# Attention scores in two fp32r parts with two heads per pass of the array, and a new order of TensorE's work

## The reference

```python
h = _layernorm(x) * (1 + ca) + sa
qkv = einsum('bsd,ed->bse', h, w_qkv) + b_qkv            # 16 heads of 16
scores = einsum('bhqd,bhkd->bhqk', q, k) / sqrt(16) + causal
attn = softmax(scores); out = einsum('bhqk,bhkd->bhqd', attn, v)
x = x + ga * (out @ w_out.T + b_out)
h = _layernorm(x) * (1 + cb) + sb
gate = h @ gate_weight.T; top1 = argmax(gate); rank = cumsum(one_hot) - one_hot   # dropped if rank >= 320
expert = gelu(dispatch @ wi) @ wo; x = x + gb * prob * expert[slot]
```

## Time and profile before

| | |
|---|---|
| median of three runs | 787.2 us (785.28 to 787.46) |
| span of the profiled execution | 782.6 us, 12208 instructions; no other time of it is given, so some 4.6 us lie around the span if it is like the median |
| first max unit, first scores unit | 41.1 us, 79.9 us |
| last max unit, last scores unit | 508.5 us, 590.9 us |
| first up matmul of the experts | 633 us |
| busy share PE, DVE, ACT, POOL | 88%, 72%, 59%, 17% |

### The profile page before, as it was taken

One profiled execution on the slowest core, in us unless ns is written; L12 is line 12 of the kernel. 1 busy time (PEld: TensorE's weight loads), 2 busy tenths in 40 slices (PEclk: granted clock), 3 DMA queues, 4 the chain that ended last, 5 costly groups with the idle time before them and its releaser, 6 DMA issues.

```text
span 782.6 us, 12208 instructions
## 1 busy us (share of the span) xinstructions
PE 689.1 (88%) x4290; PEld 367.2 (47%) x4290; DVE 561.1 (72%) x1467; ACT 459.5 (59%) x962; POOL 133.9 (17%) x194
## 2 busy tenths in 40 slices
PE   4686989999999998999999999989996279999994
PEld 3564534432323343323332323242543269999994
DVE  7754778788888787988888898960435437777762
ACT  1422445566676667766677676657783336656551
POOL 6000222220001132003310201100105300121122
PEclk9869889999999999999999999999999559999998
DMA  7436126630006033005900006000004283455200
GB/s 243 109 76 144 41 57 147 162 68 14 2 0 162 1 81 81 2 1 124 308 1 1 1 1 214 1 28 1 28 28 162 90 234 115 155 182 201 92 23 17
DMA packets 42111, 66.53 MB, mean 85 GB/s; under 512 B 3822, under 2 KB 31985, under 8 KB 41466
## 3 DMA queue, kind: packets, MB, share of 16 engines
q1 hardware_dynamic: 39746, 59.44, 27.3%
q0 software_dynamic: 2304, 6.31, 2.2%
HBM read 39.36 MB, written 26.78 MB: 85 GB/s over the span
## 4 chain that ended last, share of the span: by engine, by line
PE 74%; DVE 10%; ACT 8%; issue 4%; DMA 2%; POOL 1%; SPq 0%; DVEq 0%; POOLq 0%; ACTq 0%
PE bank L1245 17%; PE bank L1295 15%; PE bank L1325 14%; PE bank L1430 9%; PE bank L1413 8%; ACT probs L802 4%; PE bank L1187 3%; DVE chunk_max L1049 2%; PE bank L1350 2%; PE bank L1216 1%; PE bank L1396 1%; ACT qk_sb L751 1%; PE bank L1373 1%; PE bank L1228 1%; DVE stats L907 1%
## 5 line engine op out<-in xcount | busy, mean ns | idle before, releaser
L802 ACT ACTIVATE probs<-bank 128x512 f32<-128x512 f32 (+3 forms) x640 | 298.3, 537 | 124.1 <-PE bank L1325 123.0
L1049 DVE TENSOR_REDUCE chunk_max<-bank 128x1 f32<-128x512 f32 x384 | 250.7, 685 | 36.9 <-PE bank L1295 35.9
L1325 PE MATMUL bank<-stacks 104*128 104x512 bf16 (+3 forms) x640 | 195.4, 356 | 13.5 <-ACT probs L802 10.1
L1295 PE MATMUL bank<-stacks 96*128 96x512 bf16 (+3 forms) x640 | 197.7, 359 | 7.9 <-DVE chunk_max L1049 3.2
L1245 PE MATMUL bank<-probs,v_sb 128*32 128x512 f32 (+3 forms) x1280 | 151.6, 546 | 0.1
L1055 DVE CUSTOM_DVE_ANT_0 masked<-bank,causal 128x128 bf16<-128x128 f32 (+3 forms) x256 | 120.7, 484 | 15.4 <-PE bank L1295 14.6
L1295 PEld LDWEIGHTS bank<-stacks 96*128 96x128 bf16 x640 | 56.0, 98 | 160.0 <-DVE chunk_max L1049 79.4
L698 POOL TENSOR_SCALAR_AFFINE_SELECT probs<-probs 128x512 f32<-128x512 f32 x64 | 40.6, 635 | 397.4 <-ACT probs L802 397.4
L1325 PEld LDWEIGHTS bank<-stacks 104*128 104x128 bf16 x640 | 62.2, 100 | 98.7 <-ACT probs L802 65.6
L1430 PE MATMUL bank<-w_split,acts 128*128 128x256 f32 x576 | 79.9, 284 | 0.0
L1430 PEld LDWEIGHTS bank<-w_split,acts 128*128 128x128 f32 x576 | 74.5, 190 | 1.5 <-issue 0.8
(11 more groups left out here) (140 smaller groups left out, 533.6 us busy)
## 6 DMA issues: line engine op xcount, KB each, us to landing
stacks<-qk_rows SPq DMA_DIRECT2D x6, 1536.0 KB, 12.4
w_raw<-w_in SPq DMA_DIRECT2D x8, 1024.0 KB, 5.0
w_raw<-w_down SPq DMA_DIRECT2D x8, 1024.0 KB, 8.0
qk_rows<-part SPq DMA_DIRECT2D x32, 192.0 KB, 2.9
slot_rows<-empty SPq DMA_DIRECT2D x1, 5140.0 KB, 28.9
slots_sb<-slot_rows SPq DMA_DIRECT2D x8, 514.0 KB, 4.0
qk_rows<-part SPq DMA_DIRECT2D x32, 128.0 KB, 2.4
stacks<-qk_rows SPq DMA_DIRECT2D x8, 384.0 KB, 4.5
```

The costliest lines, as they stand in the source:

```text
L802: act.activation(probs[:, s % 3, h, 0:width], bank[SCORE_BANKS[u % 3]][:, 0:width], ACT.Exp)\
L1049: dve.tensor_reduce(to, src[:, 0:QB], AX.X, ALU.max).then_inc(max_read, 1)
L1295: pe.matmul(bank[MAX_BANKS[u % 3]][:, 0:width], stack(g, 0)[0:KR, h, q0:q0 + P], stack(g, 1)[0:KR, h, c * QB:c * QB + width], start=True, ...
L1325: pe.matmul(bank[SCORE_BANKS[u % 3]][:, 0:QB - lo], stack(g, 1)[0:KR + MR, h, kt * P:(kt + 1) * P], stack(g, 0)[0:KR + MR, h, b * QB + lo: ...
```

## The change

**Two parts instead of three.** q and k are split into a high part rounded to fp32r and the rest; three products (high x low, low x high, high x high) make 48 rows (KR). The maxima become two fp32 parts and 4 rows (MR) of a pair of heads, 52 rows in all.

**Two heads in the halves of the array's rows.** Heads 0 and 1 of a group lie in partitions 0 to 51 of `stacks`, heads 2 and 3 in 64 to 115. Max units are ordered so that a unit of the lower half follows one of the upper, and the heads of a score step are taken 0, 2, 1, 3.

**Shared banks.** Maxima, scores, projections, turned rows and turned heads share banks 0, 1, 2, 3, 4, 5, 7; the plan names a bank for each use, and TensorE waits for the reader of that bank's use before (`bank_free`). After the last max unit scores use banks 3, 4, 5.

**Order.** `attention_plan` is a list scheduler: it keeps modelled times for the halves of the array, the banks and the other engines, and takes the option with the lowest key; maxima and scores are emitted two at a time. Scores stay at least LAG = 60 units behind the maxima (for the first head of a step).

**Rows of maxima.** ScalarE copies the turned rows once to `row_sb`, and GpSimd's queue issues two DMAs per block that put them into the stacks (each to both heads of its half). VectorE's copy L1075 and the signal L793 are gone. The rows of ones come by 8 DMAs on SyncE instead of four ScalarE instructions.

**Rest.** The second cast on ScalarE and the second subtraction are gone; stores are four DMAs a block, loads four; SyncE follows the plan's events. `v_sb` is packed more closely.

```diff
-PARTS_Q = [0, 0, 0, 1, 1, 2]
-PARTS_K = [0, 1, 2, 0, 1, 0]
+PAIRS = HG // 2
+HEADS = (0, 2, 1, 3)
+HALF = P // 2
+PARTS_Q = [0, 0, 1]
+PARTS_K = [1, 0, 0]
-    return [[(qt, h, c) for qt in range(TB) for h in range(HG) for c in range(b + 1)] for b in range(NB)]
+    return [[(qt, 2 * a + p, c) for qt in range(TB) for p in range(PAIRS) for c in range(b + 1) for a in range(2)]
+            for b in range(NB)]
+SWITCH = 90
+VALUES_FIXED = 112
+LAG = 60
+POOL_BANKS, EARLY_BANKS, PROLOGUE_BANK = (0, 1, 2, 7, 3, 4, 5), (0, 1, 2), 7
+SCORE_BANKS = (3, 4, 5, 0, 1, 2, 7)
+LATE_SCORE_BANKS, GATE_BANKS = (3, 4, 5), (7,)
...
+    def start_of(kind, half, dep):
+        if kind == "half":
+            at = max(issued, half_free[half], dep)
+            if mode != "half":
+                at = max(at, half_free[1 - half]) + SWITCH
+        else:
+            at = max(issued, half_free[0], half_free[1], dep) + (SWITCH if mode != kind else 0)
+        return at
...
+    def emit_rows():
...
+        free[k] = read("scalar", at + 436 + TO_READER, 480) + BANK_BACK["scalar"]
+        placed[n] = free[k] + 3500
...
+    while done_steps < len(steps):
+        options = []
+        if done_max < len(maxima):
+            g, b, u = maxima[done_max]
+            if g in loaded:
+                h = units[b][u][1]
+                dep = max(free[next_bank(("max",), 1)], loaded[g], engine["vector"] - QUEUED["vector"])
+                options.append((start_of("half", h // 2, dep), 220, "vector", 2, emit_max))
+        if done_scores < len(scores):
+            n, kt, h = scores[done_scores]
+            paced = done_scores < done_max - LAG or done_max == len(maxima) or h > 0
...
+        emit = min(options, key=lambda o: (key(o), o[3]))[4]
+        emit()
+        if emit in (emit_max, emit_score):
+            emit()
...
+        if may_go_beside() and emit is emit_score and issued >= beside_at:
+            plan.append(beside.pop(0))
...
     plan += beside
-    plan.append(("weigh", weigh[0], weigh[1]))
-    plan.append(("heads_out", weigh[0]))
-    plan.append(("turn_heads", weigh[0]))
+    while waiting_heads:
+        emit_heads()
...
-        stacks = sb1("stacks", [P, 2, 2, HG, S], BF16)
+        stacks = sb1("stacks", [P, 2, 2, PAIRS, S], F32R)
...
+        def stack(g, side, h, rows):
+            return stacks[HALF * (h // 2):HALF * (h // 2) + rows, g % 2, side, h % 2, :]
...
+                if ev[0] == "max_rows":
+                    n = ev[1]
+                    g, b = divmod(n, NB)
+                    pool.wait_ge(misc_read_a, misc_reads(misc_use[ev])[0] + 1)
+                    for a in range(2):
+                        pool.dma_start(stacks[HALF * a + KR:HALF * a + KR + MR, g % 2, 0, :, b * QB:(b + 1) * QB]
+                                     .bitcast(F32),
+                                     row_sb[MR * a:MR * (a + 1), n % 2, :].bitcast(F32).rearrange("p (h s) -> p h s", h=1)
+                                     .broadcast_to([MR, PAIRS, QB])).then_inc(max_rows[n % 2], 16)
...
-                if ev[0] == "max_rows":
-
-                    n = ev[1]
-                    g, b = divmod(n, NB)
-                    rows = stack(g, 0)[KR:KR + MR, :, b * QB:(b + 1) * QB]
-                    dve.wait_ge(max_row0, n + 1)
-                    dve.tensor_copy(rows[:, 1:HG, :], rows[:, 0:1, :].broadcast_to([MR, HG - 1, QB]))\
-                        .then_inc(max_rows, 1)
...
-                    if u >= 3:
-                        pe.wait_ge(max_read, u - 2)
+                    bank_free(("max", u))
...
-                    if u >= 3:
-                        pe.wait_ge(exp_done, u - 2)
-                    pe.matmul(bank[SCORE_BANKS[u % 3]][:, 0:QB - lo], stack(g, 1)[0:KR + MR, h, kt * P:(kt + 1) * P],
-                              stack(g, 0)[0:KR + MR, h, b * QB + lo:(b + 1) * QB], start=True, stop=True)\
+                    bank_free(("scores", u))
+                    pe.matmul(bank[bank_of["scores", u]][:, 0:QB - lo], stack(g, 1, head, KR + MR)[:, kt * P:(kt + 1) * P],
+                              stack(g, 0, head, KR + MR)[:, b * QB + lo:(b + 1) * QB], start=True, stop=True)\
```

More of the change, by code:

```diff
@@ L135, in read_by @@
-    def read_by(read, rate, fixed, width, latency=60):
-        read.append(max(read[-1] if read else 0.0, now + latency) + width / rate + fixed)
+    last_of = [sum(len(units[m % NB]) for m in range(n + 1)) - 1 for n in range(NG * NB)]
+    scores = [(n, kt, h) for n in range(NG * NB) for kt in key_tiles(n % NB) for h in range(HG)]
+    steps = [(n, kt) for n in range(NG * NB) for kt in key_tiles(n % NB)]
+    first_step = {n: steps.index((n, key_tiles(n % NB)[0])) for n in range(NG * NB)}
+    last_step = {n: steps.index((n, key_tiles(n % NB)[-1])) for n in range(NG * NB)}
@@ new lines, in attention_plan @@
+    plan = []
+    started = False
+    issued = 0.0
+    half_free = [0.0, 0.0]
+    mode = "full"
+    engine = {"vector": 0.0, "scalar": 0.0, "pool": 0.0}
+    free = {n: 0.0 for n in POOL_BANKS}
+    uses = []
+    piece_bank = None
+    value_free = 0.0
+    exps_done, weigh_ready, weighed = {}, {}, {}
+    placed, rows_formed, o_taken, turned = {}, {}, {}, {}
+    waiting_rows, waiting_heads, waiting_low = [], [], []
+    loaded = {0: 0.0}
+    done_max = done_scores = done_steps = 0
+    projections = [(g, b, PROJECT_AT[g][b]) for g in range(1, NG) for b in range(NB)]
@@ new lines, in attention_plan, with next_bank, take_bank @@
+    pieces = None
+    asked = 0.0
+    loads = list(range(1, NG))
+    experts = False
+    def next_bank(key, place=0):
+        banks = POOL_BANKS
+        if done_max == len(maxima):
+            banks = LATE_SCORE_BANKS if key[0] == "scores" else GATE_BANKS
+        elif key[0] == "scores":
+            banks = SCORE_BANKS
+        elif not started:
+            banks = EARLY_BANKS
+        return sorted(banks, key=lambda n: (free[n], n))[place]
+    def take_bank(key):
+        n = next_bank(key)
+        uses.append((key, n))
+        return n, free[n]
@@ L216, in attention_plan @@
-    weigh = None
+        plan.append(("max", done_max, g, b, qt, h, c, width))
+        n, ready = take_bank(("max", done_max))
+        at = tensor("half", h // 2, ready, unit_cost(width))
+        end = read("vector", at + width / TENSOR_RATE + TO_READER, width / VECTOR_RATE + VECTOR_FIXED)
+        free[n] = end + BANK_BACK["vector"]
+        n = g * NB + b
+        if done_max == last_of[n]:
+            plan.append(("max_parts", n))
+            waiting_rows.append((n, read("vector", 0.0, 750) + 140))
@@ L219, in attention_plan, with may_go_beside @@
                ("gate_exp", 0, TAIL_TILES)]
+    beside_at = 0.0
+    def may_go_beside():
+        if done_max < len(maxima) or waiting_rows or not beside or done_scores >= len(scores) - 1:
+            return False
+        heads = sum(1 for ev in plan if ev[0] == "turn_heads") - (NG - 1) * NB
+        if beside[0][0] == "turn":
+            return beside[0][1] < TB * heads
+        return beside[0][0] != "gate" or heads == NB - 1
     plan += PROLOGUE_1
-    while maxima[len(vector)][:2] == (0, 0):
+    uses += [(("project", 0, b), PROLOGUE_BANK) for b in range(2)]
@@ L436, in layer @@
         max_parts = sem("max_parts")
-        max_row0 = sem("max_row0")
-        max_rows = sem("max_rows")
+        max_rows = [sem(f"max_rows{r}") for r in range(2)]
         scored = sem("scored")
```

575 lines of the change are left out of this document (310 added, 265 removed).

## The result

The changed kernel takes 759.3 us (median of 4 runs, 757.3 to 761.8) against 786.2 us (785.0 to 787.5) of the kernel before on the same chip: ratio 0.967, 95% interval 0.963 to 0.971. It is faster by 27 us, where 70 were forecast; 759.3 lies in the range (690 to 772), but the forecast's own case did not happen. Span 755.6 us, mean granted clock 0.898.

A forecast was written before the change was run, and what follows sets the result against it. TensorE was taken as the bound, VectorE at its heels. Prologue -3, maxima and scores together -44, scores alone -23, routing and experts 0: -70 on the span of 782.6, so 712.6, 717 us with the time around it; range 690 to 772.

The forecast's parts named there:

- the forecast's own case: Whole kernel: two halves overlap fully, weight loads stay hidden; 717 us, own range 697 to 737, chance 0.56.
- Halves side by side: Max and score units on TensorE: two run at once in the array's row halves, 108 us for 217.
- Weight loads: Stacks' fp32r loads on TensorE: 190 ns against 100 for bf16, taken as hidden behind matmuls, costing nothing.
- TensorE stops being the bound: Maxima and scores together: TensorE's work of 301 us needs 346 at 87% fill, called less than VectorE's work.
- less overlap: Rival: a unit costs 0.136 us, midway between 0.09 and 0.181; maxima and scores together 409, total 743; chance 0.18.
- -18 on VectorE: Maxima and scores together: VectorE's copy L1075 (11.3 us) and its wait (6.6) go.
- -30 of waits for TensorE: Maxima and scores together: of VectorE's 50.5 us of waiting for max matmuls, 30 go.
- Rows on GpSimd's queue: Rows of maxima by two DMAs a block: 5.4 us where the plan assumes 3.5, felt in long blocks; +4.
- Scores alone: Stage after the last max: 60 us for 83, so -23; bounds 50 and 83.
- Routing: Routing and experts after the scores: the same instructions, so 0.
- +8 for left-over tiles: End of scores alone: about 20 of 54 beside events left over, 0.4 us each.
- Start: Prologue: ScalarE's L762 and L780 go (-2.6), 8 DMAs for ones come in; together -3, from -5 to +2.

The follow-up runs named there:

- e4: Changed kernel with max and score units reordered so that both of a pair lie in the same half of the array's rows: 891.9 us, ratio 1.135.
- e7: Sliced kernel with VectorE's reductions of unmasked max units reading 256 of 512 columns, so work is left out: 741.5 us, ratio 0.945.
- sliced kernel: Also e1: changed kernel with the stacks of groups 1 to 3 loaded in four column slices, each after the one before has landed: 748.1 us, ratio 0.950.
- e8: e7 with ScalarE's exponentials of full 512-wide score units also cut to 256 columns from the 31st step on: 721.4 us, ratio 0.918.
- e10: Sliced kernel with banks not shared: three for scores, four for the other uses, as long as maxima run: 792.7 us, kernel before 785.8.
- e2: Changed kernel with two output-tile events, not one, allowed after a pair of score units: 758.3 us, ratio 0.964.
- e5: Sliced kernel with the last heads turned and divided ahead of the left-over output tiles: 744.7 us, ratio 0.947.
- e11: e5 run once more, in more rounds: 744.7 us, ratio 0.949.

## Why the prediction was wrong, step by step

*Halves side by side:* right as a mechanism. Pairs start within 0.02 us; the step from pair to pair is 0.23 to 0.24 in place of 0.22, and 0.34 behind a weigh step. The time that they are worth is not sized: the 132 us of e4 hold a lower clock as well.

*Weight loads:* right. fp32r loads of the stacks take 0.18 to 0.19 us, and inside a row of pairs they start 0.23 to 0.24 us ahead of their matmul, beside the pair that runs. Behind a weigh step they start together with their matmuls (431.47), and that pair costs 0.34.

*"TensorE stops being the bound", the first step that failed.* The sum for TensorE (301 us of work in 388) took 0.09 a unit. In the step shown, eight units take 1.55 us from the end of the weigh step, 0.19 each: 0.34 + 0.24 + 0.23 for three pairs, and 0.74 for a broken one; from 160 to 440 the mean is 0.18. At that price its sum is 193 + 1198 x 0.18 = 409 us, and from 78 to the last max it is 406.5. TensorE is at 99% from 160 on, and e7 shows that VectorE, the forecast's bound, can lose a quarter of its work for next to nothing. The comparison itself was loose as well: 346 us for TensorE is not less than VectorE's work of 331; 388 was VectorE's time with its waits. That the stretch still ran at 0.635 us a unit, near the forecast's 0.624, is luck, two errors that cancel: the unit cost twice the price, and TensorE was filled to 99% and not to the 87% taken over from before. The figure is that of the rival "less overlap", whose maxima of 409 us from 78 end at 487 (484.5 measured); its time of 743 is near the 748 of the sliced kernel, without the hole. Its mechanism came as broken pairs over late banks, not as half-overlapping halves.

*VectorE.* L1075 and its wait are gone, -18 on VectorE. The -30 of waits for TensorE did not come: 52.7 us for 50.5, and -8 from 160 us on (26.8 for 34.7). "A fixed order over shared banks also lets a late exponential hold up a maximum" was the right worry (e8), but own banks are no remedy (e10).

*Rows on GpSimd's queue: +4, the term that was mis-sized.* Issue (0.58 us each) and landing (2.2 us) were dearer in the estimate than in the trace. But the rows of three blocks fell beside a load of 3 MB each and took 8 to 16 us, and the first of them stopped TensorE; undoing that gave 11 us of time and 12 of the last max (e1). The prediction asked how long the rows take, and not what else the planner's new order puts on the DMA engines in that moment. The Trainium skill, "DMA: Bandwidth & Descriptors", section "Queues, rings and completion order", says that a DMA engine alternates between its queues packet by packet, which lets one expect small rows to slip through such a load. No run here bears that expectation out: 13.06 us beside the load, 2.2 in the median. The two row transfers landed at 139.49 and 144.87 us, each just ahead of the load issued beside it (139.90 and 145.30).

*Scores alone: -23, right in itself:* 55 us from last max to last score, forecast 58. *Routing: 0, the second step that failed.* The +8 for left-over tiles belongs to the routing's start, and there it was +22: 64.8 us from last score to first up for 42.4. Before, all 54 stood beside the 108 score units that followed the last max; beside 72 only half find room, 27 are left over for the forecast's 20, and each costs some 0.6 us for 0.4. e2 shows that their work costs about the same wherever it stands, and puts some 15 of the 22 us on them; some 3 are the order of the last heads (e5), the rest stays open. From last max to first up it is 119.8 us for 124.8 before: of the forecast's -23 only 5 are left.

*Start:* -3 to the last max was forecast for the prologue. The first max does come 5.1 us earlier (36.0 for 41.1), but at 160 us no more units have started than before. The hole stands in between, and the granted clock was 0.62 and 0.87 from 75 to 131, where the kernel before had 0.82 and 0.88; what each of them took is only known for the hole.

Sum of the misses, in the spans (755.6 for 712.6, 43 us): 21.5 us at the last max (484.5 for 463), of which the hole is 12; -3 in the scores alone; 22.4 from there to the first up; and 2 in the experts and behind them (151.3 for 149.3).

## What to carry to other kernels

When two engines stand at 87% and 85%, as before this change, taking work from the fuller one moves the time only until the next limit is reached. Here it was TensorE again, at 99% with VectorE at 90%, coupled to its readers by one strict order over shared banks: count what a unit really takes, from start to start, and halve a reader's work to see whether it counts before calling it the bound. A stage that hides side work loses its shade when it gets shorter; price the side work again. When a run is to price one part of a change, look at its granted clock before its time is believed. And when an order is planned anew, look at which large transfer now starts beside a small one that everything waits for.

## What the runs showed of the hardware

Two DMAs of 16 KB on GpSimd's queue, 2.2 us in the median, took 8.3 and 13.1 us beside 3 MB issued a quarter of a microsecond after the first of them on SyncE's queue. TensorE at 100% busy was granted 0.50 of its clock for eight microseconds (116 to 124 in e11) in the same place where another execution had 1.00; gaps lay ahead of it (5.13 of 8 us busy at 92 to 100). In e4 it was busy 79.95 of 80 us from 160 to 240 at a granted clock of 0.50 throughout, and had 1.00 from 243.5 to 424.4. A weight load for a half started while a matmul was running in that same half (431.58, the matmul of 431.47), so here loads ran beside their own half's work too.
